# Recurrent layer: the input half's differences computed by GpSimd instead of VectorE

## The reference, cut to what matters

```
xw = jnp.einsum('ntd,dh->nth', x, Wx) + b

def step(prev_h, xw_t):
    next_h = jnp.tanh(prev_h @ Wh + xw_t)
    return (next_h, next_h)
_, hs = jax.lax.scan(step, h0, jnp.swapaxes(xw, 0, 1))
```

## Time and profile before

| | |
|---|---|
| Median of three runs | 8815.31 us (8815.16 to 8830.18) |
| The profiled execution | 8899.57 us |
| Its span in the profile | 8897.8 us |
| Its mean granted TensorE clock | 0.868 |
| Busy: PE, DVE, ACT, POOL | 7059.8, 7499.4, 4330.5, 1333.4 us |

### The profile page before, as it was taken

One profiled execution on the slowest core, in us unless ns is written; L12 is line 12 of the kernel. 1 busy time (PEld: TensorE's weight loads), 2 busy tenths in 40 slices (PEclk: granted clock), 3 DMA queues, 4 the chain that ended last, 5 costly groups with the idle time before them and its releaser, 6 DMA issues. The chain is left out here.

```text
span 8897.8 us, 114093 instructions
## 1 busy us (share of the span) xinstructions
PE 7059.8 (79%) x36497; PEld 2927.5 (33%) x36497; DVE 7499.4 (84%) x12575; ACT 4330.5 (49%) x4812; POOL 1333.4 (15%) x1111
## 2 busy tenths in 40 slices
PE   5788888888888788888888882688888887964999
PEld 1333333333333333333333330222222223632653
DVE  5999999999999999999999996899999996345223
ACT  3666666666666665666666661233333332223222
POOL 0000000000000000000000000577777772000000
PEclk8899989999999998999999996899999998556559
DMA  0000000000000000000000000000000000000000
GB/s 6 1 1 1 1 1 1 1 1 1 1 1 1 1 1 1 1 1 1 1 1 1 1 1 22 18 4 4 3 3 4 4 4 2 0 8 3 0 14 5
DMA packets 14018, 28.23 MB, mean 3 GB/s; under 512 B 3665, under 2 KB 11602, under 8 KB 12434
## 3 DMA queue, kind: packets, MB, share of 16 engines
q1 hardware_dynamic: 13586, 22.47, 0.9%
HBM read 15.12 MB, written 7.34 MB: 3 GB/s over the span
## 5 line engine op out<-in xcount | busy, mean ns | idle before, releaser
L915 POOL TENSOR_TENSOR hc<-hh,cg 128x512 f32<-128x512 f32 x1024 | 1296.8, 1269 | 509.7 <-DVE hh L898 509.7
L843 ACT ACTIVATE ps_m<-ps_m,aneg 128x508 f32<-128x508 f32 x1024 | 673.4, 658 | 1191.5 <-DVE hh L898 1069.4
L898 DVE TENSOR_TENSOR_SCAN hh<-ps_m,bx 128x512 f32<-128x512 f32 x1024 | 1231.9, 1208 | 0.0
L814 PE MATMUL ps_m<-hc,pick 128*128 128x512 f32 x2048 | 1053.5, 598 | 2.1 <-POOL hc L915 0.8
L522 DVE TENSOR_TENSOR_SCAN co<-rx_d 128x772 f32<-128x772 f32 x544 | 915.2, 1744 | 0.0
L522 DVE TENSOR_TENSOR_SCAN co<-rh_d 128x3088 f32<-128x3088 f32 x128 | 843.7, 6592 | 47.5 <-ACT rh_d L378 44.8
L261 PE MATMUL r_ps<-wdiag,xsp 32*128 32x512 bf16 x3312 | 344.7, 575 | 518.3 <-DVE rh_gain L177 254.9
L880 DVE TENSOR_TENSOR bx<-ps_m,bg 128x512 f32<-128x512 f32 x1024 | 674.2, 663 | 49.0 <-PE ps_m L827 48.9
L287 PE MATMUL r_ps<-rh_s,negid 128*128 128x512 f32 x1024 | 546.0, 682 | 180.5 <-DVE rh_s L515 179.6
L316 PE MATMUL r_ps<-wdiag,whq 128*128 128x512 bf16 x2560 | 675.5, 425 | 8.7 <-DVE tq L218 8.3
L451 POOL TENSOR_TENSOR r_gate<-ident 128x1 f32<-128x1 f32 x16 | 3.5, 216 | 4514.6 <-PE r_ps L261 4514.6
(11 more groups left out here) (399 smaller groups left out, 12360.5 us busy)
## 6 DMA issues: line engine op xcount, KB each, us to landing
rows_scratch<-pc SPq DMA_DIRECT2D x48, 128.0 KB
rows<-rows_scratch SPq DMA_DIRECT2D x128, 48.0 KB
ew<-in_e SPq DMA_DIRECT2D x3, 1024.0 KB, 6.7
co<-in_x_dn SPq DMA_DIRECT2D x1, 1024.0 KB, 4.7
xcur<-in_x_dn SPq DMA_DIRECT2D x1, 1024.0 KB
out_x<-xcur SPq DMA_DIRECT2D x1, 1024.0 KB, 3.9
qi<-in_f_q SPq DMA_DIRECT2D x1, 384.0 KB, 3.3
xpw<-in_xp_t SPq DMA_DIRECT2D x1, 257.0 KB
```

What stands on the lines that cost most here:

```text
L814: e.matmul(ps[:, 6, :], pick[:, 128 - un:256 - un], hc[un % NHC][:], start=False, stop=True, skip_group_check=True).then_inc(summed, 1)
L843: e.activation(da[un % NDA][:, :, 1:T], ps[:, un % 2, :].rearrange("p (n t) -> p n t", n=NG4)[:, :, 1:T], ACT.Exp, scale=aneg[:, 0:1]).the ...
L898: e.tensor_tensor_scan(hh[un % NBUF][:], da[un % NDA].rearrange("p n t -> p (n t)"), bx[un % NBUF][:], 0.0, ALU.mult, ALU.add).then_inc(sc ...
L915: e.tensor_tensor(hc[un % NHC][:], hh[un % NBUF][:], cg[:], ALU.mult).then_inc(weighted, 1)
```

## The change

GpSimd computes the input half's differences (L518 on `rx_pd` before). The operation, its tiles and its semaphores are the same: it waits for `xs` and counts up `xd`. In the prologue, the nine differences stand between GpSimd's copies; in the loop, GpSimd's step begins with it. VectorE's list loses the instruction; nothing takes its place.

```
         @blk.gpsimd
+            def x_difference(g):
+                e.wait_ge(xs, 2 * g + 2)
+                e.tensor_tensor(X["pd"][:, :, 2:K2], X["s"][:, :, 2:K2], X["pd"][:, :, 2:K2], ALU.subtract).then_inc(xd, 1)
+
             e.wait_ge(vs, VSETUP)
             e.tensor_copy(xsp[:], xpc[:, :, 0:128]).then_inc(stp, 1)
             e.tensor_copy(xsl[:], xpc[:, :, 0:128]).then_inc(stl, 1)
+            for g in range(UN - 1):
+                x_difference(g)
             e.wait_ge(xp_mm, UN)
             e.tensor_copy(xsp[:], xpc[:, :, 128:256]).then_inc(stp, 1)
+            x_difference(UN - 1)
             e.wait_ge(xl_mm, UN)
             e.tensor_copy(xsl[:], xpc[:, :, 128:256]).then_inc(stl, 1)
+            x_difference(UN)
             with e.Fori(0, T // UN) as i:
                 for s in range(UN):
                     t = UN * i + s
+                    x_difference(t + AHEAD)
                     if s == UN - 2:
...
         @blk.vector
-            def x_difference(g):
-                e.wait_ge(xs, 2 * g + 2)
-                difference(X["pd"][:, :, 2:K2], X).then_inc(xd, 1)
-
             for g in range(AHEAD):
                 x_prefix(g)
-                x_difference(g)
                 if g:
                     x_chain(g - 1, g - 1)
...
                     tl.inc(difference(R["gain"][:], R))
-                    x_difference(g)
                     x_chain(g - 1, s)
```

## The result

The changed kernel takes 9637.62 us (median of 4 runs, 9635.78 to 9640.87), the kernel before 8822.74 us: 1.090 times the time, 95% interval 1.084 to 1.097. It is slower, inside the range given, and 123 us above the value.

A forecast was written before the change was run, and what follows sets the result against it. Each step was taken to be bound by two nearly equal paths, VectorE's and TensorE's, from the end of the state's even sums. 535 + 160 - 10 + 25 - 8 = 702 us on 8815 gave 9517, rounded to 9515 us; range 9170 to 9730.

The forecast's parts named there:

- Two paths from one point: Loop step: VectorE's and TensorE's paths both start at the state's even sums' end; freeing VectorE gains only 10 us.
- Length: GpSimd's new operation on two tensors of 2048 f32 takes 4.49 us, upper bound 5.08.
- The collision: Loop step: GpSimd gets in between state's scan and even sums, delaying the even sums 4.18 us; 535 us in all.
- The clock term: TensorE, idle longer ahead of L287, gets a lowered clock in nearly every step: 160 us, bounds 0 and 365.
- The prologue and the copies: Prologue: GpSimd delays xwt and L290, 25 us (16 to 44); 32 loop copies moved from the tanh, -8 us.
- The sum: Whole kernel: 535 + 160 - 10 + 25 - 8 = 702 us, added unscaled to the 8815 us median.
- No collision: Rival, 7 in 100: GpSimd's long operation leaves VectorE alone and the even sums keep their time; 8780 us, faster.
- GpSimd at no cost: Rival, 2 in 100: the freed VectorE has nothing to give and GpSimd costs nothing; 8815 us.
- Piecemeal handing over: Rival, 7 in 100: ports shared in pieces, VectorE's operations meanwhile take about twice their time; +290 us, 9100 us.
- One gap later: Rival, 6 in 100: GpSimd gets in between even sums and state differences, L290 waits 2.9 us; +371 us, 9190 us.

The follow-up runs named there:

- e1: Changed kernel with the input differences left out, GpSimd adding one number per partition instead: 8866.94 us, 1.0030 of the kernel before.
- e6: Changed kernel plus 24 unread matmuls on TensorE between residue and the state's L287: 9428.31 us, 1.0641 of the kernel before.
- e0: The kernel before, unchanged, run once more for a second profile: 8831.53 us, ratio 0.9985.
- e9: Changed kernel with 7 instead of 5 unread matmuls a step in the gated unit and the LSTM: 9371.13 us, 1.0591 of the kernel before.
- e8: Kernel before with 7 instead of 5 unread matmuls a step in the gated unit and the LSTM: 8640.85 us, ratio 0.9769.
- e2: Kernel before, with GpSimd also doing the same subtraction each loop step on its own tile that nobody else reads: 9450.31 us, ratio 1.0696.
- e4: Changed kernel with GpSimd's input differences cut into four instructions of four batch rows each: 9157.58 us, 1.0329 of the kernel before.
- e11: Changed kernel with the input differences split, GpSimd doing rows 0 to 7 and VectorE rows 8 to 15: 9203.80 us, 1.0424 of the kernel before.
- e5: Changed kernel, but in the loop GpSimd also waits for the state's differences before it begins: 9125.48 us, 1.0300 of the kernel before.
- e3: Kernel before, with GpSimd also doing a one-number addition and a memset of 6240 numbers each loop step: 8821.57 us, ratio 0.9971.

## Why the prediction was right

**Two paths from one point.** Right. e1 shows that VectorE's 2.29 us are hidden but for 0.27. The loop gave 34 us against my 10; 22 of them are in L287, where I had put nothing, and 12 are left.

**Length.** Right: the shortest `L441` of the profile is 4517 ns, 4.49 us by my rows. The Trainium skill (GPSIMD Engine Reference, "Performance versus the Vector engine") has 4497 ns, and the trace agrees.

**The collision.** Right in size, and in place for two steps of three. 4.13 us in the step shown, 4.18 predicted. But the sentence that GpSimd is released "when VectorE is already in the state's scan" holds in 87 of the 128 steps. In the other 41 GpSimd got in ahead of the scan, which then took some 6.5 us, and the even sums their 1.23. In all of the 41 the scan started 0.09 us or more behind the end of the input's even sums, mostly since ScalarE's copies (L407) came late; in the 87 it started at most 0.06 us behind that end, and in most of them ahead of it. The state's path loses the same either way, which was luck in so far as I hadn't looked at it. The two together, by their means over the loop:

```profile
L524 DVE TENSOR_TENSOR rh_s<-rh_s,rh_pd 128x1024 f32<-128x1024 f32 x127 | 518.6, 4083 | 4.3
...
L520 DVE TENSOR_TENSOR_SCAN rh_s<-rh_pd 128x1040 f32<-128x1040 f32 x127 | 459.7, 3619 | 13.6 <-ACT rh_pd L407 12.7
```

(4083 - 1227) + (3619 - 2319) = 4156 ns a step, where 1227 and 2319 are the two means of the kernel before; 128 times that is 532 us of the 535 predicted.

**The clock term.** Right: 184 us on L287 against 160. L290, L293 and L300 behind it take the same in both loops (456.6, 269.4 and 241.3 us for the state's). e6 took it away again.

**The prologue and the copies.** The size was near (18 us against 25), one reason was not. The prediction said that the four scans overlap, "so GpSimd gets in behind them and ahead of `xwt`". It doesn't; one turn of the prologue after the change, VectorE, then GpSimd:

```profile
139.81 11.01 DVE L531 TENSOR_TENSOR_SCAN co<-rx_d 128x772 f32<-128x772 f32 x4
```

```profile
139.98 5.92 POOL L441 TENSOR_TENSOR rx_pd<-rx_s,rx_pd 128x2048 f32<-128x2048 f32 x1 [19.25 <-DVE rx_s L524]
```

It gets in behind the first scan. As the chain ends 4.2 us later either way, the sum is the same. The 8 us for the moved copies were not measured by themselves; in the loop's means, two scans of the tanh (L163, L198) are 25 and 27 ns shorter than before, 7 us in all, and the state differences 49 ns longer, 6 us. The wrong reason rested on rows 7, where GpSimd did not get in between VectorE instructions that overlap (L191 with the one ahead of it). Those instructions take 0.33 us and the scans 1.74; why GpSimd waited past the overlap there is open.

**The sum.** 702 us predicted, 716 in the layer. Of the loop's 698, the terms give 532 + 184 - 12 = 704. Two numbers beside the sum don't hold: without the clock term it gives 8815 + 702 - 160 = 9357 and not 9330, and with heaps 80 us apart a median does not tell 18 us from no change (e0's interval runs from 0.9942 to 1.0027). The step that was missing is in the last sentence of the sum, "the terms are differences, with no reason to scale, so I add them to the median": the program has a layer whose time depends on a clock that falls early or late in it, 304 to 423 us, and all four runs of the changed kernel lie within 6 us of one another, with 422.7 us for that layer in the one that was profiled, while the median of before stands for runs with some 319. That is 104 us of the 123 by which the value was missed. e9 against e8 shows that they go when the layer's clock is held up. In the changed kernel's profile the layer runs at a mean clock of 0.91 for its first 39 us and at 0.50 from there to its end; in e0's it stays high for 271 us. Why it falls early in one and late in the other is open. It isn't the collision itself: e2 has that too, and kept the clock through the whole layer with the same fillers (304.0 us).

**The rivals.** No collision, and GpSimd at no cost: e2 and the profile exclude both. Piecemeal handing over: e4 and e11 exclude it for one instruction. One gap later, between even sums and state differences: in the changed kernel it doesn't happen, as the state differences have a mean of 2341 ns, 2292 before. No run makes it happen; e5 lets GpSimd begin only behind the state differences, and its 502 us less show what the place is worth.

## What to carry to other kernels

An instruction moved to an idle GpSimd is only free if VectorE isn't reading two SBUF tensors meanwhile: each waited for the whole of the other's instruction here, in turns, and a GpSimd instruction that only wrote cost nothing (e3). Look at what VectorE does in the microseconds after GpSimd's release, and who waits for that; the result being early is no comfort. And before a difference of medians is put down to a change, compare the stretch that was changed with itself: here an untouched layer added 100 us.

## What the runs showed of the hardware that I had not expected

- The turn between the two engines changed after one instruction, also between VectorE scans that overlap (e5: 11.34 us instead of 6.73; e4: +0.7 to +1.3 us on each of four).
- GpSimd, released at the end of the input's even sums, got in ahead of the state's scan in the 41 steps of the changed kernel in which the scan started 0.09 us or more behind that end, and in none of the 87 in which it started sooner.
- Waiting for the other engine's instruction is recorded as busy time: VectorE's busy time rose from 7499.4 to 7761.0 us with 137 instructions less.
- A subtraction on GpSimd that reads one tile twice took 3.2 us of VectorE's time, one that reads two tiles 4.1.
- With 5 filling matmuls a step, the gated unit ran at clocks from 0.54 (422.7 us, changed kernel) to 0.99 (304.0 us, e2), and the LSTM at 0.53 (481 us, kernel before). With 6 or 7 both kept 0.99, at 304 and 328 to 329 us.
